# A cross-attention and feed-forward kernel on one Trainium2 core: in the turns of the small layers, the large product is put ahead of the first layer's last matmul and the second layer's scores

## What is computed

```python
x = x + L0_xattn(layernorm(x), ctx, mask, ...)     # 32 heads of width 128, position bias, out projection
x = x + L0_ffn(layernorm(x), ...)                  # W_base, plus a mixture of 4 low-rank experts
x = x + L1_xattn(layernorm(x), ctx, Wq, bq, Wk, bk)
x = x + L1_ffn(layernorm(x), qweight, ...)         # 6-bit codes, scale and zero point per row
```

## Time and profile before

| | us |
|---|---|
| median of 3 runs | 953.75 |
| the profiled execution | 953.5 |
| its span | 951.6 |
| PE busy | 935.6 (98%) |
| DVE busy | 633.0 (67%) |
| POOL busy | 522.7 (55%) |
| ACT busy | 409.0 (43%) |

### The profile page before, as it was taken

One profiled execution on the slowest core, in us unless ns is written; L12 is line 12 of the kernel. 1 busy time (PEld: TensorE's weight loads), 2 busy tenths in 40 slices (PEclk: granted clock), 3 DMA queues, 4 the chain that ended last, 5 costly groups with the idle time before them and its releaser, 6 DMA issues.

```text
span 951.6 us, 16937 instructions
## 1 busy us (share of the span) xinstructions
PE 935.6 (98%) x5509; PEld 816.3 (86%) x5509; DVE 633.0 (67%) x1158; ACT 409.0 (43%) x1141; POOL 522.7 (55%) x583
## 2 busy tenths in 40 slices
PE   9999999999999999999999999999999999999996
PEld 8888898888889888888888888888888887877774
DVE  5675764565756676657675667567666768767876
ACT  5654535334344434443433343434343444335563
POOL 3450734476556756575657475746575654032567
PEclk9999999999999999999999999999999999999999
DMA  9224437563668466736573657456763764300001
GB/s 331 106 78 149 133 133 279 204 237 133 231 227 285 149 227 225 273 116 256 200 275 131 234 205 280 174 178 246 264 203 128 272 222 145 137 24 1 34 23 67
DMA packets 61146, 171.70 MB, mean 180 GB/s; under 512 B 6039, under 2 KB 8219, under 8 KB 60844
## 3 DMA queue, kind: packets, MB, share of 16 engines
q1 hardware_dynamic: 61100, 171.11, 50.8%
HBM read 159.56 MB, written 11.53 MB: 180 GB/s over the span
## 4 chain that ended last, share of the span: by engine, by line
PE 92%; DVE 2%; ACT 1%; POOL 1%; issue 1%; DMA 1%; SPq 0%; POOLq 0%; ACTq 0%; DVEq 0%
PE ps_q L353 7%; PE ps_q L355 7%; PE ps_q L354 7%; PE ps_o L353 6%; PE ps_o L355 6%; PE ps_o L354 6%; PE ps_k L353 6%; PE ps_t L2132 6%; PE ps_k L355 6%; PE ps_k L354 6%; PE ps_v L353 6%; PE ps_s L2105 6%; PE ps_v L355 6%; PE ps_v L354 6%; PE ps_t L2122 3%
## 5 line engine op out<-in xcount | busy, mean ns | idle before, releaser
L767 ACT ACTIVATE scores<-scores,neg_max 128x128 f32<-128x128 f32 x256 | 100.1, 393 | 219.1 <-DVE neg_max L1549 219.0
L1436 DVE TENSOR_TENSOR acc<-ps_o,acc 128x512 f32<-128x512 f32 x128 | 87.9, 687 | 65.9 <-PE ps_o L355 65.9
L353 PE MATMUL ps_o<-wo_hi,att_hi 128*128 128x512 f32 x256 | 106.0, 414 | 0.6 <-issue 0.5
L355 PE MATMUL ps_o<-wo_hi,att_lo 128*128 128x512 f32 x256 | 100.5, 393 | 0.0
L354 PE MATMUL ps_o<-wo_lo,att_hi 128*128 128x512 f32 x256 | 100.2, 391 | 0.0
L773 ACT COPY probs_t<-ps_t 128x512 f32<-128x512 f32 x64 | 37.7, 589 | 140.4 <-PE ps_t L2122 140.4
L1076 POOL TENSOR_TENSOR shift<-bias_sb,mask_sb 128x512 f32<-128x512 f32 x64 | 84.2, 1316 | 2.9 <-DVE scores L1545 2.9
L1424 DVE TENSOR_TENSOR att_lo<-ps_t,att_hi 128x512 fp32r<-128x512 f32 x64 | 44.2, 691 | 55.2 <-ACT att_hi L760 55.1
L1117 POOL TENSOR_TENSOR wq_lo<-raw_q,wq_hi 128x256 fp32r<-128x256 f32 x65 | 48.0, 739 | 59.0 <-ACT wq_hi L599 59.0
L353 PE MATMUL ps_v<-wv_hi,ct_hi 128*128 128x256 f32 x264 | 75.0, 284 | 0.1
L355 PE MATMUL ps_v<-wv_hi,ct_lo 128*128 128x256 f32 x264 | 74.7, 283 | 0.0
(11 more groups left out here) (378 smaller groups left out, 2785.1 us busy)
## 6 DMA issues: line engine op xcount, KB each, us to landing
ring_hi<-scratch_x_t SPq DMA_DIRECT2D x39, 512.0 KB, 4.0
ring_lo<-scratch_x_t SPq DMA_DIRECT2D x39, 512.0 KB, 4.9
ring_hi<-scratch_c_t SPq DMA_DIRECT2D x39, 512.0 KB, 4.1
ring_lo<-scratch_c_t SPq DMA_DIRECT2D x39, 512.0 KB, 5.3
raw_o<-in_w_o SPq DMA_DIRECT2D x16, 512.0 KB, 4.7
raw_q<-in_w_q SPq DMA_DIRECT2D x15, 512.0 KB, 6.1
raw_k<-in_w_k SPq DMA_DIRECT2D x15, 512.0 KB, 6.9
xt_hi<-scratch_x_t SPq DMA_DIRECT2D x13, 512.0 KB, 7.3
```

The lines of the kernel that those rows point to most:

```text
L353: pe.matmul(dst, hi_l, hi_r, start=first, stop=False)
L355: return pe.matmul(dst, lo_l, hi_r, start=False, stop=last)
L767: e = act.activation(probs[n][:, m, :], scores[n][:, m, :], ACT.Exp, bias=neg_max[:, n, m:m + 1], accum_out=row_sum[:, n, m:m + 1])
L1436: dve.tensor_tensor(acc[:, b, :], ps_o[:], acc[:, b, :], ALU.add).then_inc(o_added, 1)
```

## The change

On PE's queue, in every turn, the large product is put in front of `a_end(a - 1)` and `b_scores(b)` instead of behind them. Nothing else changes: no instruction is added, removed or altered, and the queues of DVE, ACT, POOL and SP are the same row for row.

```diff
@@ -2625,14 +2625,14 @@
                 if 0 <= b:
                     transpose(1, b, b_full_s)
                 transpose(0, a, a_lo_s)
+                if w < 4:
+                    product_g(4 + w)
+                if 0 <= c:
+                    c_product(c)
                 if 0 <= a - 1:
                     a_end(a - 1)
                 if 0 <= b:
                     b_scores(b)
-                if w < 4:
-                    product_g(4 + w)
-                if 0 <= c:
-                    c_product(c)
                 a_low_rank(a)
                 if 0 <= att:
                     b_attend(att)
```

## The result

The changed kernel took 957.43 us, the median of 6 runs (956.23 to 960.80); the kernel before, in the same sessions, 953.66 us. The ratio is 1.0042 with a 95% interval of 1.0029 to 1.0055: slower, as forecast, inside the range, but by 3.8 us where 8 were forecast. A later set of 5 runs of the same kernel gave 1.0066 (1.0052 to 1.0081).

What follows compares the result with a forecast made beforehand. PE was taken to bound the turns, with DVE about a microsecond behind. Delays reaching +8.3 us at `a_end(7)`, less 0.15, gave +8.1: span 951.6 + 8.1 = 959.7, plus 1.9 around it, 961.6 us; range 956.4 to 963.6.

Steps and rivals of the forecast that it cites:

- The loop: Turns 6 and 7: product, scores, b_max, z_mix, c_lo and the next product form a cycle through PE and DVE, 11.84 us.
- the waits for c_lo: Turns 5 to 7: PE waits for DVE's c_lo before the product's first L2619, 1.3 to 1.5 us each.
- the waits for z_stack: `a_end(3)` in turn 4 and `a_end(7)` in the ending wait for DVE's z_stack; they start 1.8 and 8.3 us later.
- the waits for z_mix before L2580: PE waits for DVE's z_mix before its transpose in most turns, about 1.0 us in turns 6 and 7.
- rival B: Same cycle, but alpha issues ahead of POOL's addition in turns 6 and 7, each 1.0 us shorter: 959.6 us; chance 0.22.
- DVE's own stretch from b_max to z_mix: On DVE, z_mix starts 4.36 us after b_max in turn 5 and 5.14 in turns 6 and 7, carried over unchanged.
- the collision: Turns 6 and 7: POOL's addition issues first and holds DVE's alpha to 1.25 us instead of 0.26, 1.0 per turn.
- main case: Whole kernel: the cycle through PE and DVE with alpha held up in turns 6 and 7, 961.6 us; chance 0.47.
- C: Rival: no cycle, DVE catches up and only direct waits stay, +2.9 us, 956.4 us; chance 0.12.
- D: Rival: faster, c_lo ready in time and the scores' delay absorbed, 1.8 us saved, 951.7 us; chance 0.07.
- E: Rival: worse, through more collisions (1.0 us each) or a lower clock (some 9 us), 963.6 us and up; chance 0.09.

Runs made afterwards that it cites:

- both halves of the change: Against the kernel before, the large product moved ahead only with the context (turns 0 to 3), ratio 1.0016; only with the codes (turns 5 to 7), ratio 1.0032.
- the forced collision: Changed kernel with POOL's addition moved ahead of r_diagonal in turns 6 and 7: 103.1 us of turns, +1.2; ratio 1.0069 to the kernel before.

## Why the prediction was right, and where it was too large

The loop is there, and most signs of it: the waits for c_lo (1.30, 1.15, 1.00, where 1.3 to 1.5 were named), the waits for z_stack in turn 4 and in the ending, none for `a_end` in turns 5 to 7. One sign failed: the waits for z_mix before L2580, of about 1.0 in turns 6 and 7, did not come. z_mix was over at 915.06 in turn 6, and PE came to it from its own work at 915.33; the whole wait stands before the product, for c_lo. And the period of 10.5 instead of 11.8 is by the prediction's own signs that of rival B. The delays at the anchors, forecast and measured:

| | forecast | measured |
|---|---|---|
| stage A's transposes, turn 2 | 0 | 0.0 |
| transpose of z_mix, turn 2 | +0.6 | +0.4 |
| scores, turn 4 | +2.0 | +1.5 |
| stage A's transposes, turn 6 | +3.0 | +2.2 |
| z_mix, turn 6 | +6.1 | +3.9 |
| `a_end(7)` | +8.3 | +4.8 |
| end of span | +8.1 | +4.7 |

The term that was mis-sized is DVE's own stretch from b_max to z_mix, "4.36 after b_max in turn 5 and 5.14 in turn 6". They measured 4.09 (900.17 to 904.26) and 3.88 (910.92 to 914.80). I had carried both over as DVE's own work. Two things in them were not.

First, a wait too short to be printed. In the trace before, the scaling started at 909.46, and logits came only 0.81 later:

```profile
909.26 0.97 PE L2562 MATMUL ps_k<-low_rank_in,a_full 128*128 128x36 f32 x8
909.46 0.69 DVE L1898 TENSOR_TENSOR f_scr<-ps_q,scale_rows 128x512 f32<-128x512 f32 x1
910.27 0.16 DVE L1847 TENSOR_TENSOR logits<-ps_k,logit_bias 128x4 f32<-128x4 f32 x1
```

That is when PE's low-rank product ended, at 910.23. Turns 2, 3, 5 and 7 show the same, with 0.04 to 0.05 between the two. After, the scores stand directly before low rank, low rank is over long before DVE asks, and logits follow the scaling by 0.57 (912.73 to 913.30). In turns 5 to 7 this is 0.23 to 0.24 each, in turns 2 and 3 0.18 (gg 872.14 to logits 872.78 after, 872.68 to 873.50 before): 1.1 us of the surplus of 3.4.

Second, the collision. I kept it as a fixed part of the stretch and gave its absence 0.22. The prediction said that both instructions hang on DVE's statistics in front of the scaling, at distances that do not change. That was the wrong step: the addition does follow them, at 2.08 both before and after, but alpha hangs on logits, and so on PE's low rank. It came 2.15 after the statistics before and 1.86 after the change, and so passed the addition, whose lead had been 0.07. By the rule of the Trainium skill (SBUF — State Buffer, Who interferes with whom) the first to issue keeps the other out, and the trace agrees in both directions, 0.27 ahead and 0.92 behind. For r_diagonal on POOL it did not hold to the end; that stands in the last section. The absence of the collision is the 2.0 between the main case and rival B. Both misses are of one kind: a distance between two starts was carried over as if all of it were work, and part of it was waiting for another engine.

The remaining 0.3 or so is PE's: from stage A's transposes to b_max the way grew by 2.24 us in turn 2 and by 2.18 in turn 3, where 2.35 was forecast, since the waits and restarts before the scores went.

How the number came to lie inside the range: the main case's own range, 960.6 to 962.8, does not hold it, and neither does B's 959.6. It lies within 956.4 to 963.6 because half of C had been taken in, whose mechanism is not the one found. So the number is in part luck; the direction and the loop are not. (The later set's median of 959.95 lies near B's 959.6, but the turns, which are the same in both profiles, give 4.7 and not B's 6.1.)

Against the rivals: B's case is in the trace, with its own size also 1.4 too large; C's 956.4 comes nearest to the first median only by accident, for the loop is there, and part of its 0.76 in turn 6 was c_lo's own wait of 0.46 for ACT's c_hi; D falls with the result, and both halves of the change cost time by themselves. For E, no low clock fell into the turns of the two profiles of the changed kernel; in the profile with the context product alone one did, behind the wait of 1.33 in turn 4, while both profiles of the changed kernel and that of the forced collision have the same wait and kept 1.00 there. A single instance doesn't show that the change makes it more frequent; this stays open.

## What to carry to other kernels

Filling a short wait on one engine by moving a large block ahead also delays what the block is moved past, and everything that other engines have queued behind that; ask when their queue must be back. Here 1.2 us of waits went (0.8 for z_stack in turns 1 and 5, 0.4 for b_full in turns 2 and 3), and a loop of 10.5 us per turn through two engines took the place of 9.6 on PE alone (905.30 to 914.92). Before a distance between starts is carried over to the new order, check at its start whether it coincides with the end of another engine's work; and where an instruction passes another by less than 0.1 us, price both orders of issue.

## What the runs showed of the hardware

- PE's granted clock fell to half between 830 and 840 us, while the first layer ended, in one of the two profiled executions of the changed kernel and not in the other. Of the ten profiles here seven have such a fall at that place, of 3.4 us in most; their mean clocks are 0.991 to 0.997, those of the other three 0.998 and 0.999. In the profile of the kernel before PE was busy without a gap in front of it:

```profile
826.00:834.00 8.00, 8.00 (x41) 6.54 (x41) 4.51 (x10) 3.69 (x11) 0.00 (x0) 1.00 0.93 337
834.00:838.00 4.00, 4.00 (x14) 3.18 (x14) 1.98 (x6) 1.31 (x4) 0.02 (x1) 0.58 0.08 31
```

  It cost 1.6 us: against the execution after, in which the clock stayed at 1.00 there, the same matmuls stood 0.30 us later just ahead of it (834.54 to 834.24) and 1.87 just behind it (838.18 to 836.31). That is a third of the effect that was to be measured.
- An operation of DVE on 4 columns, alpha, took 0.23 us in most turns. It took 0.92 to 1.25 where POOL's addition of 128x512 had started 0.39 to 0.07 us before it, and each time it ended within 0.03 of the addition.
- Not every operation of POOL held it to its own end. In turn 4 r_diagonal, 128x128 and 0.63 us long, started at 892.54 and alpha at 892.57; alpha took 0.36 and was over 0.24 us before r_diagonal. With r_diagonal 0.14 behind alpha, in the kernel before with DVE's order altered, it took 0.23.
